# Post-layernorm attention block with a ternary-weight feed-forward on eight cores: rework of the layernorm, quantisation and feed-forward stages

## The reference

```python
x = layernorm(x + attn(x))         # local causal attention and retrieval from 4 memories, then w_o
x = layernorm(x + ffn(x))
# ffn:
h   = act_quant(x) @ weight_quant(w_up)      # [.., 2048] x [2048, 4096]
h   = relu(h) ** 2
out = act_quant(h) @ weight_quant(w_down)    # [.., 4096] x [4096, 2048]
# act_quant:    s = 127 / max|x| of the row;  clip(round(x * s), -127, 127) / s
# weight_quant: s = mean|w|;                  clip(round(w / s), -1, 1) * s
```

## Time and profile before

| what | value |
|---|---|
| time, median of 3 runs | 4088.38 us (4085.7 to 4089.13) |
| the profiled execution | 4085.57 us |
| its span on core 5, the slowest | 4084.0 us |
| spans of the 8 cores | 4043.6 to 4084.0 us |
| busy: TensorE matmul / VectorE / ScalarE | 2377.4 / 1591.0 / 451.8 us |
| chain that ended last: TensorE / VectorE / DMA | 50% / 26% / 12% |

### The profile page before, as it was taken

The page is one execution under the profiler, slowest core; times in us unless marked ns, Lnnn a source line. Parts: engine busy times, 40 slices in busy tenths (PEclk is TensorE's granted clock), DMA queues, the critical chain, the costliest instruction groups (busy, mean ns, idle before and its releaser), DMA issues.

```text
span 4084.0 us, 38828 instructions; the slowest of 8 cores (4043.6 to 4084.0 us)
## 1 busy us (share of the span) xinstructions
PE 2377.4 (58%) x14698; PEld 1449.0 (35%) x14698; DVE 1591.0 (39%) x2793; ACT 451.8 (11%) x544; POOL 303.7 (7%) x485
## 2 busy tenths in 40 slices
PE   0467778788888878149999680144444222353532
PEld 0122243344234423048888230033333101252522
DVE  0244422222222222501111438544555766535355
ACT  0122212211221121201111001000000011000001
POOL 4000030011011000011110000000000000000000
PEclk9988888889888878579999695577777555676766
DMA  8755640111011000066651340011111000212112
GB/s 117 158 178 176 178 65 7 14 21 17 5 21 21 11 11 1 0 83 84 83 67 18 65 101 0 21 62 62 62 62 62 0 0 2 84 60 72 52 62 83
DMA packets 170027, 229.63 MB, mean 56 GB/s; under 512 B 15091, under 2 KB 129780, under 8 KB 168820
## 3 DMA queue, kind: packets, MB, share of 16 engines
q0 software_dynamic: 142864, 142.65, 19.3%
q1 hardware_dynamic: 25828, 76.10, 6.4%
q10 hardware_dynamic: 1152, 8.39, 0.5%
HBM read 294.23 MB, written 8.39 MB: 74 GB/s over the span
## 4 chain that ended last, share of the span: by engine, by line
PE 50%; DVE 26%; DMA 12%; issue 5%; DVEq 3%; ACT 3%; POOL 1%; ACTq 0%; SPq 0%; POOLq 0%
PE ps_all L732 11%; PE ps_all L1067 6%; PE ps_all L1207 6%; PE ps_all L423 6%; PE ps_all L440 5%; DMA swst<-wdnT 3%; PE ps_all L483 3%; PE ps_all L488 3%; DMA swst<-wupT 3%; DVE wub L1054 3%; DVE wdb L1194 3%; DVEq L73 3%; PE ps_all L884 3%; DVE denr L549 3%; PE ps_all L505 2%
## 5 line engine op out<-in xcount | busy, mean ns | idle before, releaser
L732 PE MATMUL ps_all<-membuf,sigT 128*128 128x256 bf16 x4096 | 449.5, 273 | 54.3 <-DMA membuf<-mem 54.3
L732 PEld LDWEIGHTS ps_all<-membuf,sigT 128*128 128x128 bf16 x4096 | 401.8, 98 | 101.7 <-issue 54.3
L1067 PE MATMUL ps_all<-wub,xqT 128*128 128x256 bf16 x2048 | 251.3, 290 | 306.4 <-DVEq L73 306.4
L1207 PE MATMUL ps_all<-wdb,rqT 128*128 128x256 bf16 x2048 | 241.5, 284 | 301.0 <-DVEq L73 301.0
L314 PE MATMUL ps_all<-xTb,wqb 128*128 128x512 bf16 x1024 | 270.8, 427 | 246.6 <-DMA wqb<-wqT 146.5
L1067 PEld LDWEIGHTS ps_all<-wub,xqT 128*128 128x128 bf16 x2048 | 211.7, 104 | 345.9 <-issue 310.3
L1207 PEld LDWEIGHTS ps_all<-wdb,rqT 128*128 128x128 bf16 x2048 | 207.7, 102 | 334.7 <-issue 302.9
L314 PEld LDWEIGHTS ps_all<-xTb,wqb 128*128 128x128 bf16 x1024 | 106.5, 107 | 410.3 <-issue 325.8
L423 PE MATMUL ps_all<-xTb,kw 128*128 128x512 bf16 x1024 | 237.6, 397 | 9.3 <-DMA kw<-wkT 9.3
L440 PE MATMUL ps_all<-vw,xTb 128*128 128x256 bf16 x2048 | 224.9, 273 | 0.0
L440 PEld LDWEIGHTS ps_all<-vw,xTb 128*128 128x128 bf16 x2048 | 200.4, 98 | 24.9
(11 more groups left out here) (134 smaller groups left out, 2360.5 us busy)
## 6 DMA issues: line engine op xcount, KB each, us to landing
swst<-wupT SPq DMA_DIRECT2D x64, 512.0 KB, 4.6
swst<-wdnT SPq DMA_DIRECT2D x64, 512.0 KB, 4.5
membuf<-mem POOLq DMA_DIRECT2D x64, 512.0 KB, 16.3
wfs<-wupT POOLq DMA_DIRECT2D x32, 1024.0 KB, 6.9
wfd<-wdnT POOLq DMA_DIRECT2D x32, 1024.0 KB, 6.4
xTb<-xT POOLq DMA_DIRECT2D x64, 128.0 KB, 9.3
wqb<-wqT POOLq DMA_DIRECT2D x16, 512.0 KB, 27.5
kw<-wkT POOLq DMA_DIRECT2D x128, 64.0 KB, 2.8
```

The lines of the kernel that those rows point to most:

```text
L732: k.emit("tensor", lambda t, ss=ss, m=m, dc=dc, bank=bank, buf=buf: t.matmul(ps[bank][:, 0:256], sigT[:, dc * OWN + ss * 128: dc * OWN + ( ...
L1067: k.emit("tensor", lambda t, ss=ss, dc=dc, bank=bank, buf=buf: t.matmul(ps[bank][:, 0:256], xqT[:, dc * OWN + ss * 128: dc * OWN + (ss + 1 ...
L1207: k.emit("tensor", lambda t, ss=ss, ic=ic, bank=bank, buf=buf: t.matmul(ps[bank][:, 0:256], rqT[:, ic * OWN + ss * 128: ic * OWN + (ss + 1 ...
```

## The change

Everything up to B2 is as it was. From B3 on:

- **Waits.** `v_emit` and `s_emit` give each instruction of VectorE and ScalarE a wait for the one before it on the same engine. The drains are gone, and `endphase()` is no longer called behind B2.
- **B3.** The residual sum goes to `x2` in bf16. ScalarE follows each piece with two activations whose accumulator gives the piece's sum and sum of squares (`pg1`, `qg1`).
- **C1.** Block by block: statistics from those sums (six operations on one column, a square root, a reciprocal), subtract and multiply in place on bf16, maximum, scale, two activations with the scale as an operand (`sciT` integer, `scq` float), two corrections, 16 transposes in two groups of 8 with one copy of 1024 columns for each, and then the 16 matmuls of slice 0 for this block. The ternary step of slices 0 and 1 stands ahead of block 0.
- **C2.** The ternary step works on 2048 columns at a time (two pairs of operations for a slice), stands ahead of the slice before in VectorE's stream, and the second half of each slice's load goes by SP's queue. The relu evacuation is ScalarE's. Row maxima are taken in pieces of 1024 columns behind every fourth slice.
- **C3.** Two activations with `Square` replace the product and the conversion, with a second set of buffers; two corrections; groups of 8 transposes. The matmuls of slices 0 and 1 of `w_down` stand between the blocks. The ternary step of slice 0 follows block 0, that of slice 1 block 1.
- **C4.** Slices 2 to 7 as before, with pieces of 2048 columns, loads in turn by POOL and SP, and four PSUM banks. ScalarE sums each piece for the second layernorm.
- **C5.** Statistics from those sums, block by block.
- Buffers have fixed addresses (`at=`) so that they can overlap.

The core of the diff:

```diff
+        def v_emit(fn, waits=()):
+            k.emit("vector", fn, waits=[(vve, last_v[0])] + list(waits),
+                   inc=vve)
+            last_v[0] = vve.n
...
-                k.emit("vector", lambda v, ss=ss, ht=ht, bank=bank, xb=xb: v.tensor_add(
-                    ybuf[:, ss * D + ht * CH: ss * D + (ht + 1) * CH],
+                ych = v_emit(lambda v, ss=ss, ht=ht, bank=bank, xb=xb: v.tensor_add(
+                    x2[:, ss * D + ht * CH: ss * D + (ht + 1) * CH],
...
+        def emit_tern_up(it):
+            buf = it % 2
+            for dh in range(2):
+                v_emit(lambda v, dh=dh: v.tensor_scalar(
+                    tnb[:, 0:2048], wfs[:, dh * 2048:(dh + 1) * 2048], -1.0,
+                    thrup[:, 0:1], ALU.mult, ALU.is_ge),
+                    waits=[up_ld[it][dh], (tmm, up_t[buf]),
+                           (vve, sw_v)])
+                tv = v_emit(lambda v, dh=dh, buf=buf: v.scalar_tensor_tensor(
+                    wub[buf][:, dh * 2048:(dh + 1) * 2048],
...
+        emit_wfs_dma(0)
+        emit_tern_up(0)
+        emit_wfs_dma(1)
+        emit_tern_up(1)
+        emit_wfs_dma(2)
...
+            ev = s_emit(lambda s, ss=ss, it=it, bank=bank: s.activation(
+                rtq[:, ss * DI + it * 256: ss * DI + (it + 1) * 256],
+                ps[bank][:, 0:256], AF.Relu, scale=f1col[:, ss:ss + 1]),
...
+        for ss in range(8):
...
+            sv = s_emit(lambda s, ss=ss: s.activation(
+                sr8[:, 40 + ss:41 + ss], sr8[:, 32 + ss:33 + ss], AF.Sqrt),
...
+            emit_c2_mm(0, ss)
...
+        for it in range(1, NCK):
+            if it + 1 < NCK:
+                emit_tern_up(it + 1)
+            if it + 2 < NCK:
+                emit_wfs_dma(it + 2)
+            for ss in range(8):
+                evac_mark[(it, ss)] = emit_c2_mm(it, ss)
...
+            flush_cells()
+            if ss < 2:
+                adv_dn((ss + 1) * 4)
+            emit_c4_mm(0, ss)
+            if ss >= 1:
+                emit_c4_mm(1, ss - 1)
...
+        for ht in range(2, 8):
+            adv_dn((ht + 1) * 4)
             for ss in range(8):
...
+                emit_c4_mm(ht, ss)
+                flush_cells(keep=1)
```

More of the change, by code:

```diff
@@ L897, in build_program @@
-                xo_v[xb] = vve.n
-            wo_t[buf] = tmm.n
[L899 to L934, removed]
-            vv = vve.n
-            k.emit("scalar", lambda s: s.activation(sr8[:, 32:40],
-                                                    sr8[:, 24:32], AF.Sqrt),
-                   waits=[(vve, vv)], inc=sse)
-            stat_s[0] = sse.n
-            k.emit("vector", lambda v: v.reciprocal(sr8[:, 40:48],
-                                                    sr8[:, 32:40]),
-                   waits=[(sse, stat_s[0])], inc=vve)
-            k.drain("vector", inc=vve)
-            return vve.n
@@ L1021, in build_program @@
[L1021 to L1029 removed]
+                    waits=[(tmm, womm), (s_xo[xb], xld)])
+                bank_guard[bank] = (vve, ych)
+                xo_v[xb] = ych
@@ L1084, in build_program @@
+        x2_v = last_v[0]
         if dbg:
@@ new lines, in emit_tern_dn_idx @@
+        def emit_tern_dn_idx(idx):
+            ht, qb = divmod(idx, 4)
+            buf = ht % 2
+            sb_ = idx % 2
+            extra = [(tmm, c2_last)] if ht < 2 else []
+            v_emit(lambda v, sb_=sb_: v.tensor_scalar(
+                tnb[:, 0:2048], wfd[sb_][:, 0:2048], -1.0,
+                thrdn[:, 0:1], ALU.mult, ALU.is_ge),
+                waits=[(s_dn[sb_], dn_ld[idx]), (tmm, dn_t[buf])] + extra)
+            tv = v_emit(lambda v, qb=qb, sb_=sb_, buf=buf: v.scalar_tensor_tensor(
+                wdb[buf][:, qb * 2048:(qb + 1) * 2048],
+                wfd[sb_][:, 0:2048], thrdn[:, 0:1],
+                tnb[:, 0:2048], ALU.is_ge, ALU.subtract))
+            tern_prev[idx] = tv
+            if qb == 3:
+                terndn_v[ht] = tv
@@ new lines, in build_program, with emit_c4_mm @@
+        pend_cells = []
+        cell_k = [0]
+        def emit_c4_mm(ht, ss):
+            kk = cell_k[0]
+            cell_k[0] += 1
+            bank = 4 + kk % 4
+            buf = ht % 2
+            wts = [(vve, terndn_v[ht]), (vve, rq_done[ss])] + bank_w(bank)
+            for ic in range(NCI):
+                k.emit("tensor", lambda t, ss=ss, ic=ic, bank=bank, buf=buf: t.matmul(
+                    ps[bank][:, 0:256],
+                    rtq[:, qbase(ss) + ic * 128: qbase(ss) + ic * 128 + 128],
+                    wdb[buf][:, ic * 256:(ic + 1) * 256],
+                    start=(ic == 0), stop=(ic == NCI - 1)),
+                    waits=wts if ic == 0 else (),
+                    inc=tmm if ic == NCI - 1 else None)
+            pend_cells.append((ht, ss, bank, tmm.n))
@@ L1222, in build_program @@
-        y2_v = vve.n
+                wts_ci = [(sdbg, dbg_gate3),
+                          (vve, rq_hist[step - 2] if step >= 2
+                           else last_v[0])]
+                s_emit(lambda s, o0=o0, ss=ss, sci_=sci_: s.activation(
+                    sci_[:, 0:2048], rtq[:, o0:o0 + 2048], AF.Square,
+                    scale=sc3[:, ss:ss + 1]), waits=wts_ci)
+                sqv2 = s_emit(lambda s, o0=o0, ss=ss, scq_=scq_: s.activation(
+                    scq_[:, 0:2048], rtq[:, o0:o0 + 2048], AF.Square,
+                    scale=sc3[:, ss:ss + 1]))
```

582 lines of the change are left out of this document (319 added, 263 removed).

## The result

The changed kernel takes 3375.29 us in the median of 8 runs (3371.05 to 3387.78), the kernel before 4087.49: a ratio of 0.826, 95% interval 0.825 to 0.827. In some executions of every kernel one die or both run at a lower granted clock and are longer (4161 and 4291 us in two of the eight of before); all ratios, and all times given for the experiments, leave such executions out. The forecast was 3392 with a range of 3345 to 3450. The profiled execution took 3378.9 us, 3377.3 of them the span.

The account below looks back on a forecast made before the run. It took the kernel to be bounded by VectorE's order and per-operation cost, not matmuls. From B3's end at 2431.7 us, eight steps through C5 reach a span of 3387.7, scaled to 3392 us; range 3345 to 3450.

Parts of the forecast that it names:

- Step 1: Ternary step of slices 0 and 1 after B3: four pairs, 15.4 us, and 3.5 for slice 1's first half.
- Step 2: C1: each block a chain of 22.8 us, the square root behind the evacuation; eight blocks 181.3 us.
- Step 3: C2, slices 1 to 15: TensorE runs on at the high clock, 211 us, after 3.5 for slice 0's matmuls.
- Step 4: Between C2 and C3: last maxima, 13 small operations, root and two activations, 10.4 us.
- Step 5: C3: two ternary steps of 18.6 us, blocks 3 to 7 at 19.85 each, 189.3 us in all.
- Step 6: After C3: three remaining blocks of matmuls, 12.5 us, then slice 2's ternary step, 18.8 us.
- Step 7: C4, slices 2 to 7: ternary pairs behind the seventh block's evacuation, period 46.1 us, 260.9 in all.
- Step 8: C5: rest 2.1 us, eight blocks of 5.3, and 5.4 to the end of the span.
- Loads taking over: C2 and the ternary steps: two queues slow landings to about 16 us, giving 3556 us; chance 0.07.
- The low clock in C3: C3: TensorE stays at the low clock, 64 matmuls take 13.5 us, not 9, giving 3426; chance 0.12.
- Full overlap in C4: C4: ternary step hidden under the matmuls, period 30.4 us or less, giving 3312; chance 0.03.
- SP with pieces of 1 KB: SP's loads in C2 and C4: kernel slower than before if a transfer takes 38 us or more; chance 0.01.

Follow-up runs that it names:

- Experiments 4: Changed kernel with C2's next ternary step put back behind the current slice's matmuls: 3513.0 and 3519.6 us, ratio 0.860 to the kernel before.
- experiment 5: Changed kernel with each ternary pair cut into eight of 256 columns, order kept: 3589.8 and 3592.0 us, ratio 0.879 to the kernel before.
- Experiment 1: Changed kernel with C3's Squares ahead of the finished blocks' sums on ScalarE, and their wait loosened in step 1: 3354.7 and 3357.3 us.
- Experiment 2: Changed kernel with C4's four ternary quarters spread behind the first, third, fifth and seventh block's evacuations: 3282.3 and 3288.7 us, ratio 0.803.
- the two kernels built on before: The kernel before itself, and the same with only its ternary step widened to 2048 columns: the latter 3789.5 and 3797.5 us, ratio 0.928.
- experiment 7: Changed kernel with all loads of w_up and w_down by SP's queue, none by POOL: 3359.7 to 3366.8 us, ratio 0.823 to the kernel before.

## Why the prediction was right, and where not

From the end of B3 the changed kernel took 964.6 us (2412.7 to 3377.3); by the forecast's steps it is 956.0 (2431.7 to 3387.7; the terms as written add up to 956.5, the ends were carried on 0.5 lower). Step by step:

- **Step 1**, 18.9: measured 18.7, right.
- **Step 2**, 181.3 with blocks of 22.8: measured 174.5 with blocks of 22.0. The chain was the forecast's. Timeline of the changed kernel:

```profile
2455.60 0.47 ACT L1024 ACTIVATE rtq<-ps_all,f1col 128x256 bf16<-128x256 f32 x1 [11.43 <-PE ps_all L1016]
2456.22 0.20 ACT L1051 ACTIVATE sr<-sr 128x1 f32<-128x1 f32 x1
2456.52 0.16 DVE L1054 RECIPROCAL sr<-sr 128x1 f32<-128x1 f32 x1 [3.17 <-ACT sr L1051]
2456.79 0.75 DVE L1057 TENSOR_SCALAR x<-x,sr 128x2048 bf16<-128x2048 bf16 x1
```

  The root does follow the evacuation. The terms off were small: bf16 to bf16 takes 0.753 us, the lower bound and not the 1.0 that I chose (2 x 0.25 a block), and the gaps 0.1 and not 0.14. The copy of 1024 took 0.692, forecast 0.68.
- **Step 3**, 3.5 + 211: measured 214.1 behind C1's last copy. Right, and the step with the largest share of the gain. Experiments 4 and 5 show what it rests on: the place of the ternary step and the width of its pieces.
- **Step 4**, 10.4: 10.0.
- **Step 5**, 189.3: 201.8, the step that failed. "ScalarE (4.2) works ahead on the other buffers" is true of its buffers but not of its queue. From block 3 on a period was 22.35 us, not 19.85: five times 2.5 is the 12.5 us missing. TensorE's restart with 64 matmuls was about rightly priced, 8.4 to 9.6 us against 9; the mistake was to price the path through TensorE, and not to follow ScalarE's stream from `flush_cells` to the Squares. Experiment 1, which moves those instructions, gives 19.4. That blocks 0 to 2 with their two ternary steps came to 90 us as forecast is luck, for errors cancel there. Block 0 took some 4 us more, for the Squares of its second step waited for the first step's copies. Each ternary step took 0.4 to 1 us more. Block 2 took some 5 us less: the forecast had 64 matmuls ahead of its transposes, but slice 0's matmuls for block 1 had run during the ternary step, and only the 32 of slice 1 were left:

```profile
2905.18 5.11 PE L1225 MATMUL ps_all<-wdb,rtq 128*128 128x256 bf16 x32 [13.37 <-DVE wdb L1188]
```

- **Step 6**, 12.5 + 18.8: 12.0 and 20.6, and 0.7 ahead of it. The ternary step waited 5.2 us for its third quarter's load, where the forecast's sum leaves 3.
- **Step 7**, period 46.1, 260.9 in all: 265.5. The idle time ahead of a slice in the changed kernel, first and last of five (16.1 to 18.0 us in all):

```profile
3111.27 30.60 PE L1225 MATMUL ps_all<-wdb,rtq 128*128 128x256 bf16 x256 [16.35 <-DVE wdb L1188]
...
3300.98 29.63 PE L1225 MATMUL ps_all<-wdb,rtq 128*128 128x256 bf16 x256 [16.21 <-DVE wdb L1188]
```

  The forecast had 15 to 16 us, released by VectorE: it holds but for 1 to 2 us, with periods 1.3 us longer, (3300.98 - 3111.27) / 4 = 47.4. Experiment 2 shows that place in the order is all that is behind them.
- **Step 8**, 49.9: 46.7; the gaps of the one-column operations again.

So two errors of opposite sign, C3 at +12.5 us against C1 at -6.8 and C5 at -3.2, with 6.6 more for steps 6 and 7, left 8.6 us on the steps themselves; that they cancel so far is luck. The median came out lower than forecast, not higher, because the part ahead of B3's end was 19 us earlier than in the profiled execution of before. The forecast took that part as unchanged. Most of it is the wait ahead of B1's matmuls. Their row in the groups of before:

```profile
L732 PE MATMUL ps_all<-membuf,sigT 128*128 128x256 bf16 x4096 | 449.5, 273 | 54.3 <-DMA membuf<-mem 54.3
```

and of the changed kernel:

```profile
L742 PE MATMUL ps_all<-membuf,sigT 128*128 128x256 bf16 x4096 | 450.1, 274 | 39.4 <-DMA membuf<-mem 39.4
```

In the mean over cores `w_o`'s first matmul is 12 us earlier (2299.3 to 2287.0), and the other 7 are scatter of the slowest core. The 12 are not chance: the two kernels built on before agree to 1.1 us, and those built on the changed one lie at 2281.5 to 2288.0. Between the first issue of `membuf` and TensorE's first matmul on it lay 51.7 us before and 36.8 after, both at up to 150 GB/s, in which that queue moved 7.2 MB and 4.6 MB. The difference is in every run: in the mean over cores the wait ahead of these matmuls is 45.4 and 43.2 us in the two kernels built on before, and 32.6 to 34.8 in all that have the change. By the text, which is the same, the first matmul waits for the first eight loads in both, 8 x 512 KB = 4.2 MB. So in the kernel before some 3 MB of the loads behind them were moved before these eight were complete, and in the changed one 0.4. Why wasn't tried and stays open.

**The rivals.** Loads taking over: in C2 the DMA share was 0.41, near the 0.45 foreseen, and landings were 6.4 to 6.8 us, not 16. The low clock in C3: 64 matmuls took 8.4 to 9.6 us, not 13.5, so it did come back each time. Full overlap in C4: not in the changed kernel, but experiment 2 gained some 90 us where the rival priced 80. SP with pieces of 1 KB: 6.4 to 6.7 us, and 5.4 when alone, far from 38.

**The rule against the change.** POOL's DMA instruction took 1.32 us in the median beside compares of 2048 columns, 0.884 beside those of 256 in experiment 5, and 0.884 in experiment 2, where most stand beside an evacuation: 0.44 more, once 0.79. The Trainium skill, "SBUF — State Buffer", the "DVE blocks DMA" trap, foresees such a delay; its direction agrees with these rows and its size here is about a third of the 1.3 us that I took from it. The 16 us less idle time of experiment 7 are more than it can give: eight times 0.44 is 3.5 us, by my estimate. For bf16 on both sides the Trainium skill, "VectorE: DVE Perf Modes", The perf-mode tier table, gave 693 ns; the row has 753 with a pointer as the scalar, and by 693 C1 would have been 1 us shorter still. The page was nearer than my value between the bounds.

## What to carry to other kernels

Each engine runs its stream in order, so an engine that is free and whose buffers are free can still be late: for each operation on the path, read what stands ahead of it in its own engine's stream and what that waits for. Here three such places, none of which changed a single operation, were worth 20 us (4 of them by a wait that was wider than needed), 24 and some 90. And a preparing step belongs where TensorE still has matmuls of the slice before to do. In C2, where the evacuations are ScalarE's, it can stand ahead of that whole slice; in C4, where they are VectorE's, it was spread between them. 141 us in C2 and some 90 in C4 hang on that place alone. Whether standing ahead of the whole slice would do in C4 wasn't tried.
